# Weighting pairs of edge rows after their sum instead of before it, in a two-layer graph network kernel

## The reference

```python
out = x @ root + bias
for r in range(8):                                   # relations
    mask = (edge_type == r)
    sums = segment_sum(x[src] * mask[:, None], dst)  # over 20000 edges
    cnt  = segment_sum(mask, dst)
    out  = out + (sums / maximum(cnt, 1)[:, None]) @ weight[r]
u = out
z = concatenate([u, x], axis=1) @ w_gate + b_gate
h = tanh(u) * z + x * (1 - z)
x = layernorm(x + h)

h   = x @ W                                          # second layer
out = segment_sum(h[src] * (dinv[src] * dinv[dst])[:, None], dst) + b
x   = layernorm(x + relu(out))
```

## Time and profile before

| | |
|---|---|
| median of 3 runs | 1665.67 us (1658.63 to 1668.82) |
| the profiled execution's own time | 1663.41 us |
| its span, first to last instruction | 1661.6 us |
| mean granted TensorE clock | 0.989 of full speed |
| message loops, run 0 | about 730 to 1019 us |
| message loops, run 1 | about 1035 to 1345 us |

### The profile page before, as it was taken

How to read it: one execution, slowest core, us unless ns; L and a number is a source line. 1 busy time by engine, 2 the same in 40 slices (tenths; PEclk the granted TensorE clock), 3 DMA queues, 4 the chain that set the end, 5 groups by cost and what they waited for, 6 DMA issues and landing times.

```text
span 1661.6 us, 23836 instructions
## 1 busy us (share of the span) xinstructions
PE 1612.4 (97%) x7947; PEld 1310.1 (79%) x7947; DVE 1120.2 (67%) x1885; ACT 682.9 (41%) x1239; POOL 713.1 (43%) x649
## 2 busy tenths in 40 slices
PE   8999999999999999999999999899999996999997
PEld 7888888888877777788788878688877885788886
DVE  4856655665366676657877874778777857676586
ACT  3211111111178888635555553555555652222100
POOL 1000777777600000057677663767676604322000
PEclk9999999999999999999999999999999997999999
DMA  6322435344312122277677774766768774755743
GB/s 232 107 84 101 114 104 141 103 128 122 93 63 72 59 69 70 104 227 229 209 230 225 214 215 165 229 204 211 232 209 265 280 260 147 262 212 207 274 163 115
DMA packets 122124, 280.34 MB, mean 169 GB/s; under 512 B 23142, under 2 KB 24406, under 8 KB 121872
## 3 DMA queue, kind: packets, MB, share of 16 engines
q0 software_dynamic: 38256, 104.17, 21.7%
q1 hardware_dynamic: 46912, 98.19, 18.4%
q10 hardware_dynamic: 36832, 76.44, 12.3%
HBM read 209.97 MB, written 83.10 MB: 176 GB/s over the span
## 4 chain that ended last, share of the span: by engine, by line
PE 91%; DVE 3%; ACT 2%; issue 2%; DMA 1%; SPq 0%; ACTq 0%; POOL 0%; DVEq 0%; POOLq 0%
PE PG L789 64%; PE PG L978 6%; PE PG L1044 5%; PE PG L885 3%; PE PM L812 3%; PE PM L813 3%; PE PM L801 3%; PE PG L951 2%; DMA ROWS_HI<-y 1%; PE PM L847 1%; ACT TALLY L1142 1%; PE PM L830 1%; PE PM L960 0%; ACT SRCFAR L1114 0%; PE PM L771 0%
## 5 line engine op out<-in xcount | busy, mean ns | idle before, releaser
L789 PE MATMUL PG<-WHI,XHI 128*128 128x512 f32 x1600 | 635.7, 397 | 3.5 <-DVE WLO L1322 2.2
L789 PE MATMUL PG<-WHI,XLO 128*128 128x512 f32 x1600 | 626.3, 391 | 2.9 <-issue 2.8
L789 PE MATMUL PG<-WLO,XHI 128*128 128x512 f32 x1600 | 625.8, 391 | 1.2 <-issue 1.2
L789 PEld LDWEIGHTS PG<-WHI,XLO 128*128 128x128 f32 x1600 | 301.7, 189 | 68.0 <-issue 4.3
L789 PEld LDWEIGHTS PG<-WHI,XHI 128*128 128x128 f32 x1600 | 302.1, 189 | 67.2 <-issue 4.1
L789 PEld LDWEIGHTS PG<-WLO,XHI 128*128 128x128 f32 x1600 | 302.1, 189 | 63.1 <-issue 2.6
L1094 ACT ACTIVATE STAGE<-PG 128x512 f32<-128x512 f32 x200 | 119.0, 595 | 451.8 <-PE PG L789 378.6
L1322 DVE TENSOR_TENSOR WLO<-WRAW,WHI 128x512 fp32r<-128x512 f32 x176 | 121.6, 692 | 216.6 <-ACT WHI L1087 169.5
L702 POOL DMA_INDIRECT WORK<-y,REC x184 | 207.7, 1129 | 103.0 <-issue 55.0
L702 POOL DMA_INDIRECT RAW<-y,REC x184 | 206.0, 1120 | 86.0 <-issue 53.4
L660 POOL DMA_INDIRECT records<-RREC,IDX x160 | 210.2, 1313 | 61.0 <-issue 43.7
(11 more groups left out here) (266 smaller groups left out, 2319.8 us busy)
## 6 DMA issues: line engine op xcount, KB each, us to landing
y<-STAGE ACTq DMA_DIRECT2D x220, 256.0 KB
WRAW<-in_L_gnn_weight_dram SPq DMA_DIRECT2D x128, 256.0 KB
EDGE_ROWS<-edge_rows POOLq DMA_DIRECT2D x10, 1000.0 KB
WRAW<-in_L_gnn_w_gate_dram SPq DMA_DIRECT2D x32, 256.0 KB
WORK<-y SPq DMA_DIRECT2D x15, 512.0 KB, 4.3
WORK<-x SPq DMA_DIRECT2D x10, 512.0 KB, 4.6
WORK<-in_x_dram SPq DMA_DIRECT2D x9, 512.0 KB, 3.6
XROWS<-in_x_dram SPq DMA_DIRECT2D x9, 512.0 KB
```

The lines of the kernel that those rows point to most:

```text
L789: last = pe.matmul(PG[:, bank, :], lhs[:, k, t * P:(t + 1) * P], rhs[:, j % 2, k, :], start=(k == 0 and n == 0), stop=(k == KT - 1 and n = ...
```

## The change

With weights a (even row x) and b (odd row y) the kernel before computes ax and then ax + by. The changed kernel stores b/a in place of b (`weight_ratios`, once, with a held above 1e-6), VectorE adds x + (b/a)y, ScalarE multiplies by a while it makes the high part, and VectorE multiplies by a again while it subtracts for the low part. `scale_row` and its semaphore are gone; `msg_sum` waits for both rows itself.

```diff
+TINY = 1e-6
+        INVERSE = place("INVERSE", [P, NPAIR], F32, "split_lo")
-            def scale_row(pair, slot, run):
-                act.wait_ge(got[2 * slot], 16 * (run * NPAIR // SLOTS + pair // SLOTS + 1))
-                nc.scalar.activation(raw[2 * slot], raw[2 * slot], ACT.Copy,
-                                     scale=REC[:, 2 * pair, 1:2].bitcast(F32)).then_inc(row_scaled, 1)
-
             def msg_high(pair, slot, run):
                 act.wait_ge(pair_summed, run * NPAIR + pair + 1)
                 after(act, pair_done, run * NPAIR + pair + 1 - SLOTS)
-                nc.scalar.activation(sp_hi[:, slot, :], raw[2 * slot + 1], ACT.Copy).then_inc(msg_hi, 1)
+                nc.scalar.activation(sp_hi[:, slot, :], raw[2 * slot + 1], ACT.Copy,
+                                     scale=REC[:, 2 * pair, 1:2].bitcast(F32)).then_inc(msg_hi, 1)
 
             def message(pair, run):
-                if pair == 0:
-                    scale_row(0, 0, run)
-                if pair + 1 < NPAIR:
-                    scale_row(pair + 1, (pair + 1) % SLOTS, run)
                 msg_high(pair, pair % SLOTS, run)
+            def weight_ratios():
+
+                weights = REC[:, :, 1].bitcast(F32).rearrange("p (n e) -> p n e", e=2)
+                link(V.tensor_scalar(INVERSE[:, :], weights[:, :, 0], TINY, None, ALU.max))
+                link(V.reciprocal(INVERSE[:, :], INVERSE[:, :]))
+                link(V.tensor_tensor(weights[:, :, 1], weights[:, :, 1], INVERSE[:, :], ALU.mult))
...
             def msg_sum(pair, slot, run):
+                dve.wait_ge(got[2 * slot], 16 * (run * NPAIR // SLOTS + pair // SLOTS + 1))
                 dve.wait_ge(got[2 * slot + 1], 16 * (run * NPAIR // SLOTS + pair // SLOTS + 1))
-                dve.wait_ge(row_scaled, run * NPAIR + pair + 1)
...
             def msg_low(pair, slot, run):
                 dve.wait_ge(msg_hi, run * NPAIR + pair + 1)
-                V.tensor_tensor(sp_lo[:, slot, :], raw[2 * slot + 1], sp_hi[:, slot, :].bitcast(F32),
-                                ALU.subtract).then_inc(msg_split, 1)
+                V.scalar_tensor_tensor(sp_lo[:, slot, :], raw[2 * slot + 1], REC[:, 2 * pair, 1:2].bitcast(F32),
+                                       sp_hi[:, slot, :].bitcast(F32), ALU.mult, ALU.subtract).then_inc(msg_split, 1)
...
             last.then_inc(rows_free, 1)
+            weight_ratios()
             start_sums(0)
```

More of the change, by code:

```diff
@@ L348, in gnn_resnorm_kernel @@
         got = [sem(f"got{b}") for b in range(2 * SLOTS)]
-        row_scaled = sem("row_scaled")
         pair_summed = sem("pair_summed")
```

## The result

The changed kernel took 1671.66 us (median of 10 runs, 1669.22 to 1675.26). The kernel before, run beside it on the same chip, took 1665.14 us (median of 10 runs, 1658.63 to 1668.82). The ratio is 1.0043, with a 95% interval of 1.0028 to 1.0059: slower by 0.4%, about 7 us. (This ratio and those of the experiments are the ones on record, with their intervals; they are not the quotients of the medians, here 1.0039, and can differ from them by up to 0.2%.) That is inside 1% and inside the range of the forecast, but it is not "no change": the interval leaves out 1. The profiled execution took 1670.66 us, with a span of 1668.9 us against 1661.6 us before, 7.3 us more.

What follows compares the result with a forecast made beforehand. TensorE was taken to bound the kernel. The terms, -0.8 us at the head of run 1, +0.14 at that of run 0 and +0.15 at three other waits, gave -0.5 us: 1665 us, range 1653 to 1672 us.

Steps and rivals of the forecast that it cites:

- What bounds the kernel: TensorE, busy 1612.4 of 1661.6 us; the change can directly win at most its 7.5 us of waits before L812.
- Part 1: Removing 184 row scalings of 719 ns, 132 us of ScalarE, is by itself worth nothing; TensorE never idles in the regular window.
- Part 2: ScalarE's high part grows from 630 to 719 ns, hidden behind VectorE's one-hot and addition except in a run's first three pairs.
- Part 3: VectorE's low part grows from 695 to 745 ns, 9.2 us over 184 pairs; counts only where TensorE waits for it.
- Part 4: Three VectorE operations ahead of run 0, 1.0 to 1.3 us, hidden behind the bias copy's DMA wait: 0.
- Part 5: Head of run 1: without scalings the first pairs' path shortens, TensorE's 4.62 us wait shrinks; -0.8 us, bounds 0 and 1.0.
- +0.14 us at the head of run 0: Loss at the start of run 0, where the first high and low parts are open.
- The one on the slower side: VectorE cannot catch up after signal hold-ups, if the low part costs 0.6 us more than taken; 1694 us, 3%.
- all waits for messages would go: All five TensorE waits before L812, 7.5 us, and the clock's fall go: -11 us or more, with luck 1652 us; 5%.
- the clock stay up: Head of run 1: the shorter wait might not bring the clock's fall, which cost 3.0 us; -3.5 us, 1662 us; 15%.
- the last rival: Rows land so late at the head of run 1 that the -0.8 is gone, +0.3 stays: 1666 us; 20%.
- Within 1%: The forecast of 1665 us and the clock and late-row rivals lie inside 1% of no change: together 92%.

Runs made afterwards that it cites:

- e2: Kernel before with one edit: the high part copied with a scale of ones, 724 against 630 ns; 1677.19 us, ratio 1.0050.
- e4: Changed kernel with the low part as a plain two-input subtraction, without the weight; 1675.71 us, ratio 1.0061 to the kernel before.
- e17: Kernel before plus one tiny one-column ScalarE operation behind the high part's signal; 1675.50 us, ratio 1.0080.
- e18: Kernel before plus three tiny ScalarE operations behind the high part's signal; 1677.99 us, ratio 1.0084.
- e3: Kernel before with the row scaling left out, the sum waiting for both gathers itself; 1663.55 us, ratio 0.9997.
- e14: Kernel before plus a tiny VectorE operation (59 ns) ahead of the low part's wait; 1661.79 us, ratio 0.9984.
- e13: e5 plus a tiny VectorE operation (59 ns) ahead of the low part's wait; 1678.04 us, ratio 1.0078 to the kernel before.
- e7: e2 with the scaled high part cut to 384 of 512 columns, all but the first four pairs; 1666.79 us, ratio 1.0000 to the kernel before.
- e8: Changed kernel with the high part cut to 384 of 512 columns, all but the first four pairs; 1663.56 us, ratio 0.9984 to the kernel before.
- e1: Kernel before with one edit: the low part made by the three-input operation with a scale of ones; 1664.28 us, ratio 0.9989.
- e16: Kernel before with two tiny ScalarE operations between the high part and its signal; 1671.17 us, ratio 1.0032.
- e6: Kernel before with three tiny two-column ScalarE operations between the high part and its signal; 1668.92 us, ratio 1.0024.
- e5: Kernel before with one tiny one-column ScalarE operation behind the unscaled high part, which raises its signal; 1680.76 us, ratio 1.0092.
- e15: Changed kernel plus a tiny VectorE operation ahead of the low part's wait; 1671.77 us, ratio 1.0034 to the kernel before.
- e11: Changed kernel with VectorE's low part of a pair put one pair later; 1667.55 us, ratio 1.0077 to the kernel before.
- e12: Kernel before with VectorE's low part of a pair put one pair later; 1666.06 us, ratio 1.0061.
- e9: Kernel before with every gathered row cut to 128 of its 512 numbers; 1649.54 us, ratio 0.9974.

## Why the prediction was right or wrong, step by step

**What bounds the kernel: right on the place, wrong on what reaches it.** TensorE's waits were the place to look. But I took only its 7.5 us before L812 as open to the change, and said that the gaps in products have "nothing to do with messages". They are 5.2 us before and 10.1 to 15.6 us in e2, e4, e17 and e18 together with their longer or added operations behind the sum; in the changed kernel itself, with 3.3 us, they did not grow, so its loss does not lie in them.

**Part 1, the scaling is worth nothing: right.** e3: ratio 0.9997 (0.9981 to 1.0012). ScalarE's total fell by 102.7 us where I had written 116: the rows' lengths add to 115, but neighbours on ScalarE overlap, and the engine's busy time counts the overlap once.

**Part 2, the high part gets a scale: this step failed.** The length was right (724 ns against 719). That "it hides behind VectorE's own work" was worked out from the lengths of the one-hot and the addition, 0.9 us in all. These rows overlap too; the low part starts 0.79 us behind the high part, and the longer operation puts that to 0.83, so the cover was in truth 0.03 to 0.04 us short in the regular course. That slip is not what cost, though: e14 has VectorE's low part as late as e13 and loses nothing, and in e17 and e18 it is not late at all and they lose 0.8%. What I had priced at nothing, without a reason beyond the 45% of ScalarE's time that is free, is what the added time does to the operations that follow the high part on ScalarE: they start 0.63 us behind it instead of 0.54. e2 measures it alone: +0.5% for 0.094 us a pair, about 8 us of the time for 17 us of an operation's length that no wait of TensorE names. In e7 and e8, without the added length, it is gone. That this place costs is shown; how it reaches TensorE is not.

**Part 3, the low part's third input: right on its cost, 753 ns against 745, and on its being hidden.** e1: 0.9989 (0.9976 to 1.0003). VectorE's total is 1133.2 us, forecast 1130. In e4 the changed kernel is not faster without it.

**Part 4, the ratios: right.** They run from 711.73 to 713.01 us, and the copy behind them still waits for its DMA, as VectorE's timeline shows; the forecast was a wait of 1.1 to 1.4 us:

```profile
711.73 0.14 DVE L1529 TENSOR_SCALAR INVERSE<-REC 128x92 f32<-128x92 f32 x1
711.91 0.73 DVE L1530 RECIPROCAL INVERSE<-INVERSE 128x92 f32<-128x92 f32 x1
712.67 0.34 DVE L1531 TENSOR_TENSOR REC<-REC,INVERSE 128x92 f32<-128x92 f32 x1
714.32 4.95 DVE L1635 COPY WORK<-WORK 128x4608 f32<-128x4608 f32 x1 [1.31 <-DMA WORK<-in_L_gnn_bias_dram]
```

**Part 5, the head of run 1: right in sum, in part by luck.** VectorE's timeline there, to be held against the earlier trace rows:

```profile
1041.18 0.75 DVE L1555 SCALAR_TENSOR_TENSOR WORK<-WORK,REC 128x512 f32<-128x512 f32 x1 [14.68 <-DMA WORK<-y,REC]
...
1042.73 0.75 DVE L1562 SCALAR_TENSOR_TENSOR SPLO<-WORK,REC,SPHI 128x512 fp32r<-128x512 f32 x1 [0.59 <-ACT SPHI L1125]
...
1044.08 0.75 DVE L1555 SCALAR_TENSOR_TENSOR WORK<-WORK,REC 128x512 f32<-128x512 f32 x1 [0.60 <-DMA WORK<-y,REC]
...
1045.62 0.75 DVE L1562 SCALAR_TENSOR_TENSOR SPLO<-WORK,REC,SPHI 128x512 fp32r<-128x512 f32 x1 [0.59 <-issue]
...
1050.32 4.95 DVE L1635 COPY WORK<-WORK 128x4608 f32<-128x4608 f32 x1
1056.06 0.69 DVE L1569 TENSOR_TENSOR WORK<-WORK,PM 128x512 f32 x1 [0.79 <-issue]
1056.78 0.75 DVE L1562 SCALAR_TENSOR_TENSOR SPLO<-RAW,REC,SPHI 128x512 fp32r<-128x512 f32 x1
```

The low part of pair 0 starts 1.55 us behind the sum of pair 0, before 1.93: 0.38 sooner, forecast 0.41. The second sum waits for its rows for 0.60 us, the bound that I had named. With it the low part of pair 1 comes 4.44 us behind the first sum, before 5.06, and the copy 9.14 us, before 9.59: 0.62 and 0.45 sooner, where the forecast was 1.05 and 0.85. The low part of pair 3 starts 15.60 us behind the first sum, before 16.39: 0.79 sooner, forecast 0.8. But only 0.45 of that came the way I had worked out. The other 0.34 came behind the copy, where the addition stood for 0.79 us instead of 1.14, which was in no term. It is worth little in a kernel that comes to this place 3.8 us later; TensorE's longest wait before L813 is 4.2 us, before 4.6, forecast 3.8.

**The sum: wrong by the term of part 2.** Forecast -0.5 us, measured about +7 us; the part that was missing is e2's +0.5%. The small terms can't be checked at this size: for the +0.14 us at the head of run 0 the first pair came at 732.2 us instead of 732.5, and in e1, e3, e7 and e14 it comes anywhere from 731.2 to 733.6. That 1671.66 us lies inside the forecast's range is the width of that range and not its working.

**The rivals.** The one on the slower side had VectorE fail to catch up after held-up signals, and wanted a low part 0.6 us longer. It names a sight that came true, more waits behind such signals (9 instead of 5 before L813), with the wrong engine behind it: VectorE's longer pair cost nothing in e1, and its unchanged course did not help e17. That all waits for messages would go did not happen, nor did the clock stay up at the head of run 1, though the wait there was shorter (columns as in the earlier trace rows):

```profile
1055.00:1063.00 8.00, 5.36 (x13) 4.24 (x14) 6.87 (x13) 2.44 (x4) 4.34 (x5) 0.58 0.50 163
```

The granted clock is 0.58 in these 8 us, against 0.62 in those of the earlier trace rows. Rows landing late did hold the second sum for 0.60 us, as the last rival had it, but took away only a part of the gain. "Within 1%" was the right case; that it would be no change at all was not.

**What stays open.** How ScalarE's added time gets to TensorE. The runs exclude VectorE's waiting for the high part, the low part's lateness and the scaled form, and the bytes of the gathers for the greater part. They don't give a rule for the size: e16 (two operations ahead of the signal, 1.0032) and e6 (three, 1.0024) cost less than e5 (one, 1.0092) and less than e18 (three behind it, 1.0084). Whether each small shift moves the episodes of late signals in its own way was not tried. Nor was a rival that the traces offer: in the kernel before, from 700 to 1400 us, a DMA queue that they call `q8 instruction` moves 23 blocks of 16 KB, one every 30 us or so. Waits of VectorE or ScalarE of over 1 us that end "remote" come about as often, some two dozen of them from 771 to 1285 us. In e18 such a block starts at 1267.0 us, 1.4 us ahead of the episode shown, but that from 925.5 to 932.4 us lies 4 us from the nearest one. No run varied these transfers, so they are neither shown to matter nor ruled out.

## What to carry to other kernels

A free share of an engine's time is no proof that an operation on it may grow. In this kernel, 0.1 us per pair at one place of an engine that is 41% busy cost 0.3 to 0.9%, while 0.72 us per pair taken off the same engine at another place gave nothing. So in a pipeline as full as this one leave room for a few tenths of a per cent to the slower side when an operation on a hidden engine grows; that much is a rule of thumb from one kernel. When one edit is to be judged, put it alone into the kernel before, and next to it a run in which only its length is undone (e2 and e7 here): the two are edits of a line or two, and they settled which edit costs, which no reading of the trace had. Compute cover from the distance between starts, not from the sum of lengths: 0.79 us here where the lengths say 0.9 or more.

## What the runs showed of the hardware

- TensorE's late signals and the gaps in its products can come together, as in the episode of e18: matmuls 0.7 or 1.4 us apart, and signals held up by up to 5.6 us for two engines at once. What holds them isn't named by any row.
- GpSimd's busy time, of which the 368 gathers of message rows are some 413 us in the kernel before, goes with the loss. It is 713.1 us before and 712.9, 711.9, 713.2, 714.0 and 713.6 us in e1, e3, e14, e7 and e8, which lose nothing; it is 702.5 us in the changed kernel and 697.3 to 704.5 us in e2, e4, e5, e13, e15, e17 and e18. The gathers' instructions are a little shorter in the slow kernels (1.12 us in the mean before, 1.10 in the changed one). This is only seen, not explained. e16 with 708.3 us and a loss of 0.32% lies between, and e6 with 722.8 us and a loss of 0.24% doesn't fit in, nor do e11 and e12 (718.3 and 718.7 us, 0.77 and 0.61%).
- An operation of ScalarE on one column is 186 ns long by its row but moves the next one by 0.10 us only (0.63 instead of 0.53 us from the start of the high part), since neighbours overlap.
- The same kernel took 1654.7 us on the chip of e9 to e12 and 1663.7 to 1667.4 us on the others.
